# Transposes of sums moved from TensorE to VectorE, a separate list for block loads, and the split maxima turned later in the step

## The reference

```python
x = x + _L0_xattn_ref(_layernorm(x), ctx, ctx)       # gelu(x ctx^T) ctx, 1601 rows of ctx per batch
x = x + _L0_ffn_ref(_layernorm(x), Wg, W1, W2)       # 8 experts of 512, each token to one of them
x = x + _L1_xattn_ref(ctx, _layernorm(x), mask, Wq, Wk, Wv, Wo, rel_bias)
x = x + _L1_ffn_ref(_layernorm(x), Wp1, ..., Wo, bo) # one expert per batch, chosen from its last row
```

```python
q = (dst @ Wq.T).reshape(B, T_q, H, D_K)             # H = 16 heads of D_K = 16
scores = einsum('bqhd,bkhd->bhqk', q, k) + bias
scores = where(mask, scores, -1e9)
out = einsum('bhqk,bkhd->bqhd', softmax(scores), v).reshape(B, T_q, H * D_K)
return out @ Wo.T
```

## Time and profile before

| | |
|---|---|
| median of 3 runs | 728.78 us (727.0 to 732.06) |
| the profiled execution | 730.0 us |
| its span | 728.1 us |
| TensorE busy | 652.9 us (90%) |
| VectorE busy | 336.9 us (46%) |
| ScalarE busy | 272.0 us (37%) |
| mean clock of TensorE | 0.966 of full |

### The profile page before, as it was taken

The page is one execution under the profiler, slowest core; times in us unless marked ns, Lnnn a source line. Parts: engine busy times, 40 slices in busy tenths (PEclk is TensorE's granted clock), DMA queues, the critical chain, the costliest instruction groups (busy, mean ns, idle before and its releaser), DMA issues.

```text
span 728.1 us, 9151 instructions
## 1 busy us (share of the span) xinstructions
PE 652.9 (90%) x3116; PEld 392.0 (54%) x3117; DVE 336.9 (46%) x1093; ACT 272.0 (37%) x375; POOL 97.1 (13%) x101
## 2 busy tenths in 40 slices
PE   3999999999997767999976899999999989899996
PEld 2666666666664446999864333334334334344644
DVE  4324423003026872232236776777777767323302
ACT  1111111111121330434305576675775766752220
POOL 0000000000020002445520613000102300303000
PEclk9999999999998996999989899999999989999999
DMA  9992205203001135122254760560462000402031
GB/s 310 361 361 99 95 1 169 77 0 120 0 1 63 35 106 152 50 65 66 78 149 56 104 88 2 80 99 27 79 93 62 3 2 2 117 1 59 5 110 59
DMA packets 48100, 61.98 MB, mean 85 GB/s; under 512 B 7927, under 2 KB 41240, under 8 KB 47656
## 3 DMA queue, kind: packets, MB, share of 16 engines
q1 hardware_dynamic: 45944, 55.66, 29.3%
q0 software_dynamic: 2112, 5.77, 2.8%
HBM read 43.89 MB, written 10.93 MB: 75 GB/s over the span
## 4 chain that ended last, share of the span: by engine, by line
PE 71%; DVE 14%; issue 5%; DMA 5%; ACT 3%; POOL 1%; POOLq 0%; DVEq 0%; ACTq 0%; SPq 0%
PE ps L860 13%; PE ps L871 12%; PE ps L1430 7%; PE ps L1412 5%; PE ps L1300 5%; PE ps L1132 4%; PE ps L1123 3%; DVE arena L2122 3%; PE ps L1028 3%; DVE arena L1830 2%; PE ps L944 2%; PE ps L1142 2%; PE ps L1020 2%; PE ps L1097 2%; PE ps L1333 2%
## 5 line engine op out<-in xcount | busy, mean ns | idle before, releaser
L2122 DVE TENSOR_REDUCE arena<-ps 128x1 f32<-128x400 f32 x256 | 130.9, 566 | 49.7 <-PE ps L1300 49.0
L1652 ACT ACTIVATE arena<-ps 100x1024 f32<-100x1024 f32 x128 | 124.3, 1022 | 57.4 <-PE ps L1412 57.2
L860 PE MATMUL ps<-xnT,arena 128*128 128x512 f32 x208 | 102.0, 616 | 0.9 <-DVE xnT L1715 0.9
L871 PE MATMUL ps<-arena 128*128 128x256 f32 x416 | 98.5, 381 | 0.0
L871 PEld LDWEIGHTS ps<-arena 128*128 128x128 f32 x416 | 79.6, 191 | 32.8 <-issue 24.5
L1475 ACT ACTIVATE arena<-ps 128x512 f32<-128x512 f32 x52 | 31.0, 597 | 174.9 <-PE ps L860 174.9
L1300 PE MATMUL ps<-arena 97*128 97x400 bf16 x256 | 76.4, 342 | 6.3 <-ACT xnT L1613 2.0
L1412 PE MATMUL ps<-arena 100*100 100x512 bf16 x256 | 77.7, 388 | 1.1 <-DMA arena<-arena 0.6
L1430 PE MATMUL ps<-arena 100*32 100x512 f32 x512 | 70.6, 615 | 0.2 <-ACT arena L1652 0.2
L1300 PEld LDWEIGHTS ps<-arena 97*128 97x128 bf16 x256 | 20.4, 97 | 78.7 <-DVE arena L2122 38.9
L1715 DVE COPY xnT<-ps 128x512 f32<-128x512 f32 x16 | 10.4, 686 | 100.9 <-PE ps L833 100.9
(11 more groups left out here) (228 smaller groups left out, 717.4 us busy)
## 6 DMA issues: line engine op xcount, KB each, us to landing
arena<-in_W SPq DMA_DIRECT2D x16, 512.0 KB, 9.1
arena<-in_ctxT SPq DMA_DIRECT2D x4, 1664.0 KB, 7.9
arena<-in_ctxN SPq DMA_DIRECT2D x4, 1664.0 KB, 12.9
arena<-arena SPq DMA_DIRECT2D x48, 128.0 KB
arena<-in_pW SPq DMA_DIRECT2D x8, 512.0 KB, 4.4
last_k_parts<-arena SPq DMA_DIRECT2D x24, 100.0 KB, 1.8
arena<-last_k_parts SPq DMA_DIRECT2D x8, 300.0 KB
x_tok<-in_x SPq DMA_DIRECT2D x4, 512.0 KB, 9.3
```

Of the source, the lines that this page charges most:

```text
L860: ins = pe.matmul(ps[:, 4 + k % 2, :], ctxT_s[:, b % 2, c, f * P:f * P + P], xnT[:, c, S * b:S * b + S], start=(c == 0), stop=(c == KC - 1))
L871: ins = pe.matmul(ps[:, b % 2 * 2 + t // 2, t % 2 * D:t % 2 * D + D], hid[:, (k - 2) % 4, t * P:t * P + P], ctxN_s[:, b % 2, f, :], start= ...
L1652: act.activation(pexp2[0:KT, c % 4, :, :], ps[0:KT, 2 + 2 * (c % 2):4 + 2 * (c % 2), :], ACT.Exp).then_inc(f_pe, 1)
L2122: dve.tensor_reduce(nm2[:, h, j:j + 1], ps[:, FAST.bank(x), 0:KF], AX.X, ALU.max, negate=True).then_inc(s_by["dve"], 1)
```

## The change

1. **Sums.** In `fast_way` VectorE now transposes the sums itself, in squares of 32 x 32 elements, straight from bank 6 into `vt2`, in the first step of the next unit. One square is a head's 32 rows by 32 queries, so the sum of exponentials of a query ends up beside its values. In the second step it divides into `vn2`, and in the third step of every second unit it transposes 128 x 512 of them back into `xnT`. The copies by ScalarE, the transposes on TensorE and the turning of the finished batch ("turn", "last turn") go; `WoT` is laid out for the new order of columns on the host. The batch is projected at steps 3 and 4, its roots begin at step 4, and "turn4" stands at 10 and 12.
2. **Maxima.** The split maxima are transposed at the end of the second step, behind its sum product and its last two maxima products, instead of ahead of the sum product. ScalarE takes them last in the step.
3. **Experts.** The list of tokens to load is made by itself after the block transposes (`s_idxl`); GpSimd issues each load as soon as that block is turned, then the stores. `s_ysd` goes; the engines wait for the stores themselves. A row of zeros is stored once ahead of the loop. SyncE loads the first keys only after the first four gathers (`s_xsb` 64).
4. **Threshold.** One of the key products stands behind the transpose of the threshold.
5. **End of attention.** The last batch's projection stands ahead of the first answers of the fourth block, on TensorE and on VectorE.

The general way (`near > 0`), which these inputs don't take, is adapted to the new order of columns.

```diff
-CHAIN = {3: ("turn", 0), 4: ("turn", 1), 7: ("project", 0), 8: ("project", 1), 12: ("turn4", 0), 15: ("turn4", 1)}
+CHAIN = {3: ("project", 0), 4: ("project", 1), 10: ("turn4", 0), 12: ("turn4", 1)}
+ROOTS_AT = 4
...
-    if t == 1 and u + 1 < UNITS:
-        found.append(("max rows", u + 1))
-    if t == 2 and u >= 1:
-        found.append(("values", u - 1))
...
+def rows_of_step(st):
+
+    u, t = divmod(st, CT)
+    return u + 1 if t == 1 and u + 1 < UNITS else None
...
             sp.wait_ge(s_ekst[0], 48 * KC * B // 2)
+            sp.wait_ge(s_xsb, 64)
             for half in range(2):
                 keys(0, half)
...
-                last_keys(3 + r)
+                if r + 1 < ROUNDS:
+                    last_keys(3 + r)
             pe.wait_ge(s_soft, 3)
             pe.transpose(ps[:, 0, 0:P], kept[:, CAND:CAND + 1].broadcast_to([P, P]), eye).then_inc(s_prT, 1)
+            last_keys(2 + ROUNDS)
...
                         max_products(maxima_of_step(st, 2, HG))
+                        if rows_of_step(st) is not None:
+                            turn_maxima(rows_of_step(st))
...
-                part4_hidden(0, 0, 2)
-                turn_values(UNITS - 1)
-                part4_hidden(0, 2, FC)
+                part4_hidden(0, 0, FC)
+                pe.wait_ge(f_oc, UNITS)
                 route_logits(FAST, 1)
                 pe.wait_ge(s_acc_f, B)
-                pe.wait_ge(f_oc, UNITS)
-                for k in range(KC):
-                    turn_piece(FAST, ("last turn", B - 1, k))
                 pe.wait_ge(f_pe, 2 * STEPS)
+                project(B - 1, 4)
                 reasoned(0, 0)
-                for k in range(KC):
-                    taken(FAST, ("last turn", B - 1, k))
-                project(B - 1, 4)
                 reasoned(0, 1)
...
-                    act.wait_ge(s_ysd, i + 1)
+                    act.wait_ge(s_ys, i * 32 + 16)
...
-                    if st % CT == 0 and st > 0:
-                        take_values(st // CT - 1)
...
+                dve.wait_ge(s_xsTr, i * 2 + 3)
+                dve.tensor_scalar(idx_x[:, :], idx[:, bass.ds(i * 2 + 4, 2)], 0.0, None, ALU.add).then_inc(s_idxl, 1)
                 for j in range(2):
                     dve.wait_ge(s_xsTr, i * 2 + j + 3)
                     dve.tensor_copy(xsT[:, j, :, :].rearrange("p k n -> p (k n)"), ps[:, 6 + j, 0:KC * P]).then_inc(s_xsT, 1)
-                dve.tensor_scalar(idx_x[:, :], idx[:, bass.ds(i * 2 + 4, 2)], 0.0, None, ALU.add)
-                dve.wait_ge(s_ysd, i + 1)
+                dve.wait_ge(s_ys, i * 32 + 16)
                 dve.tensor_scalar(idx_y[:, :], idx[:, bass.ds(i * 2, 2)], 0.0, None, ALU.add).then_inc(s_idx, 1)
...
+                def turn_values(i):
+
+                    dve.wait_ge(f_pv, CT * (i + 1))
+                    dve.transpose(vt2[:, i % 2, :, :].rearrange("p a v -> p (a v)"), ps[:, 6, :]).then_inc(f_oc, 1)
+
                 def normalise(i):
 
-                    b, g = divmod(i, NG)
-                    x = ("values", i)
-                    dve.wait_ge(s_made, FAST.made(x))
-                    v = ps[:, FAST.bank(x), :].rearrange("p (j h v) -> p j h v", j=TB, h=HG)
-                    cf.step(dve, dve.reciprocal(rl2[:, :, :, :], v[:, :, :, DK:DK + 1]))
-                    dve.tensor_tensor(xn[:, TB * b:TB * b + TB, g * HG * DK:(g + 1) * HG * DK].rearrange("p t (h d) -> p t h d", d=DK),
-                                      v[:, :, :, 0:DK], rl2.broadcast_to([P, TB, HG, DK]), ALU.mult).then_inc(s_by["dve"], 1)
...
+                    lo = i % 2 * DK
+                    dve.wait_ge(f_oc, i + 1)
+                    cf.step(dve, dve.reciprocal(rl2[:, :, :], vt2[:, i % 2, :, DK:DK + 1]))
+                    cf.step(dve, dve.tensor_tensor(vn2[:, i // 2 % 2, :, lo:lo + DK], vt2[:, i % 2, :, 0:DK],
+                                                   rl2.broadcast_to([P, S // VW, DK]), ALU.mult))
+
+                def turn_back(i):
+
+                    b, k = divmod(i // 2, KC)
+                    ins = dve.transpose(xnT[:, k, S * b:S * b + S], vn2[:, k, :, :].rearrange("p a v -> p (a v)"))
...
+                    if t == 0 and u >= 1:
+                        turn_values(u - 1)
+                    if t == 1 and u >= 1:
+                        normalise(u - 1)
+                    if t == 2 and u >= 1 and u % 2 == 0:
+                        turn_back(u - 1)
...
-                        n = st - (b + 1) * NG * CT - 7
+                        n = st - (b + 1) * NG * CT - ROOTS_AT
...
             with pool.Fori(0, pairs) as i:
+                pool.wait_ge(s_idxl, i + 1)
+                pool.sem_inc(s_turn, 1)
+                for j in range(2):
+                    pool.wait_ge(s_xsTr, i * 2 + j + 3)
+                    pool.sem_inc(s_turn, 1)
+                    load_tokens(j, idx_x[:, j:j + 1])
                 pool.wait_ge(s_idx, i + 1)
                 pool.sem_inc(s_turn, 1)
-                for j in range(2):
-                    load_tokens(j, idx_x[:, j:j + 1])
...
-                pool.wait_ge(s_ys, i * 32 + 32)
-                pool.sem_inc(s_ysd, 1)
```

More of the change, by code:

```diff
@@ L183, in maxima_of_step @@
     return range(min(first + lo, UNITS * MU), min(first + hi, UNITS * MU))
-TAKER = {"max": "dve", "max rows": "act", "values": "dve", "queries": "act", "products": "act", "turn": "act", "project": "dve",
-         "turn4": "act", "route": "act", "logits": "dve", "last turn": "dve", "last turn4": "dve"}
+TAKER = {"max": "dve", "max rows": "act", "queries": "act", "products": "act", "project": "dve",
+         "turn4": "act", "route": "act", "logits": "dve", "last turn4": "dve"}
 LAST_TURNS = [(("last turn4", B - 1, 0), 6), (("last turn4", B - 1, 1), 7), (("route", 2), 6), (("logits", 2), 4)]
@@ L214, in fast_pieces @@
             yield ("max", m), next(turns), TAKER["max"]
-    for name, bank in [(("route", 1), 7), (("values", UNITS - 1), 7), (("logits", 1), 6), (("last turn", B - 1, 0), 6),
-                       (("last turn", B - 1, 1), 7)] + LAST_TURNS:
+        if rows_of_step(st) is not None:
+            yield ("max rows", rows_of_step(st)), next(turns), TAKER["max rows"]
+    for name, bank in [(("route", 1), 7), (("logits", 1), 6)] + LAST_TURNS:
         yield name, bank, TAKER[name[0]]
@@ L555, in _ @@
         def _(sp):
-            for s_free in (s_ysd, s_kst, s_mr):
+            for s_free in (s_kst, s_mr):
                 sp.sem_inc(s_free, 1)
@@ L2204, in fast_way @@
                         split_maxima(u + 1)
+                turn_values(UNITS - 1)
                 normalise(UNITS - 1)
+                turn_back(UNITS - 1)
                 route_shift(FAST, 1)
-                for k in range(KC):
-                    take_turned(FAST, ("last turn", B - 1, k))
-                answers(0, 0)
                 choose(1)
                 project(B - 1, 4, 1)
+                answers(0, 0)
                 answers(0, 1)
```

62 lines of the change are left out of this document (25 added, 37 removed).

## The result

The changed kernel takes 747.26 us, the median of four runs (745.93 to 748.77), against 728.5 for the kernel before on the same chip: the ratio is 1.025 (95% interval 1.0209 to 1.0291). It is slower, by far more than the 1% that a measurement can tell, and outside the range of 710 to 728. The profiled execution has a span of 745.8 us, 17.7 more than the one before.

What follows compares the result with a forecast made beforehand. TensorE was taken to set the attention loop's pace, VectorE not far behind; the expert head waits for a gather. Terms -6.3 - 2.9 + 1.3 - 1.8 = -9.7 gave 719 us for the median, range 710 to 728.

Steps and rivals of the forecast that it cites:

- (a): Head of expert stage: gather freed from key loads, start 3.7 us earlier, first hidden products 2.6 us shorter; -6.3 us.
- (b): Expert loop: fetch list made and loads issued earlier, so nine passes take 67.5 us instead of 70.4; -2.9 us.
- (c): Threshold turned before a key product: the product delays the prefix sums by what the threshold gained; 0.
- (e): End of attention: the last sums' turning and last rows' transposes with their wait leave TensorE; -1.8 us.
- (d): Attention loop: turning moved from TensorE to VectorE; +2.1 us at full clock, -0.8 for the clock, +1.3 us in all.
- The walk: Step-by-step queue timing of attention: clean unit 12.2 us against 11.97, batch 56.9 against 55.0; sum +2.8, less 0.7.
- the crowd: Unit with the second projection: first step 5.1 us on VectorE against TensorE's 4.4; TensorE stands still 1.9 us.
- the clock: Rival: three long TensorE waits each bring several us at 1.2 GHz, more near the router; attention +9, whole 727; chance 0.10.

Runs made afterwards that it cites:

- e1: Kernel before with only parts 3 and 4 of the change (experts, threshold), attention loop untouched: ratio 0.993 to the kernel before.
- e2: Changed kernel with the second projection, statistics, roots and turned rows of a batch spread over more steps: ratio 0.9949 to the kernel before.
- e9: As e5, with GpSimd's additions to the first batch's rows moved behind those of the second: ratio 0.9745 to the kernel before.
- e10: As e9, with SyncE loading the first keys only after eight gathers instead of four: ratio 0.9762 to the kernel before.
- e3: Changed kernel with filler products on TensorE at its waits in the unit of the second projection: ratio 1.0156 to the kernel before.
- e4: Changed kernel with GpSimd's two additions per batch cut to one column of 256 (result not the reference's): ratio 1.0073 to the kernel before.
- e5: As e2, with late queries one step and their products two steps earlier, and a GpSimd wait ahead of its additions: ratio 0.9812 to the kernel before.
- e6: Kernel before (TensorE turns sums) with the change's expert stage and threshold, maxima's transposes behind the sum product, late products earlier: ratio 0.9891 to the kernel before.
- e8: The changed kernel run again, code identical: ratio 1.023 to the kernel before.
- e11: Changed kernel with projections, roots and turned rows at their old steps: ratio 1.0136 to the kernel before.
- e7: Kernel before with only the maxima's transposes moved behind the sum product: ratio 0.9959 to the kernel before.

## Why the prediction was wrong

- **(a) Head, -6.3.** Half right. The start moved by 4.4 us (3.7 forecast). The first hidden products took 5.44 us, not 3.7, at a clock of 0.69: the fall came with the shorter wait too in this execution, as in e1, e2, e9 and e10, and not in e3, e4, e5, e6, e8 and e11 (3.81 there). I had read the fall of the kernel before as one that came while TensorE waited; it came right behind: the clock was 1.00 from 281 to 285 us and 0.64 in the two us after. And "I take nothing" for the key loads meeting the first pass's gathers was wrong: 1.43 us here, up to 3.5 in others. By the third pass 3.7 us were left (301.04 against 304.74).
- **(b) Passes, -2.9.** Right in this execution: from the third pass to the end of the last answers 60.4 us against 62.8, -2.4. It did not come again: the same code took 64.7 us in e8, and e7, with the old expert stage on the same chip, 65.4. In e8 and every other run with this expert stage some passes took 8.3 or 8.4 us with an idle time of 0.5 at their start that the profile puts down to no wait; why, is open.
- **(c)** nothing seen, as said. **(e) -1.8:** right, -1.6.
- **(d) Attention, at full clock.** The walk was good: clean unit 12.08 for 12.2, transposes 0.717 for 0.69 to 0.71, the crowd where it was put. The second batch of e8, which has no fall, took 56.0 us, where the walk had 56.9 and the kernel before takes 54.9; its longest wait of TensorE was 1.39 us, not 1.9. e7 came out to 0.1 us, with a stretch of 3.4 us at 1.2 GHz gone besides, and e9's loop 3 us under the walk's 208 for its table of steps. Over the whole loop the 2.1 us that it forecast as lost at full clock are not to be seen in the balance below.
- **(d) Attention, the clock.** The step that failed is "I count two clock falls of 1.2 us: +2.4 - 3.2 = -0.8". Against what the same steps take in e4, e5 and e8 the changed kernel loses 6.1 us at steps 8 to 10, 4.5 at 20 to 22, 3.4 and 7.8 in the third batch (the second of these is GpSimd's), 4.5 at 52 to 54 and 3.0 at the end, 29.3 in all; less the 3.2 us that the kernel before itself lost that makes 26.1 of the 25.6 measured, so the queues at full clock cost about nothing in sum. About 6 of the 29.3 are the three waits for GpSimd themselves (1.47, 2.78 and 1.74 us), an estimate, and the other 23 the clock. Both factors were wrong. The **price** of a fall is 4.5 us, not 1.2: no row gives 1.2, and the kernel before lost 3.2 at two short stretches of 6.8 and 3.4 us, 1.6 each, while in five of the six places here the clock stayed low for 10 to 14 us. And the **number** was six, not two: the crowd that I foresaw gave three, and three more came because the waits at them had a cause that I didn't have, VectorE's small operations held until GpSimd's instruction ended.
- The prediction has no term for GpSimd at all: what its instructions do to VectorE's stood at nothing without a reason. The rival named "the clock" had the mechanism, with "several us" for each long wait, and the size of +9 for it was a third of what came. Its price of 727 was 20 us too low. The sign of GpSimd's part was in the trace of before: in the unit at 452 us the casts of the split took 0.59 and 1.01 us beside GpSimd's, for a TensorE wait of 1.20.

## What to carry to other kernels

Where TensorE is busy nine tenths of the time, a wait of 1.4 us, or two of 0.54 and 0.74 close together (at 625 us), can cost 4.5 us of clock, and need not (e3, e8); so ask of a change that moves work to another engine which are the longest waits that it makes in one place, not what it adds to the sum. List the small operations of VectorE whose duration varies, and lay GpSimd's instructions over them in the timeline: an engine for which nobody waits can still hold the chain. Filler products in a suspected wait are a cheap test of whether the clock or the queue is what costs.

## What was not expected of the hardware

- Of the 31 stretches at 1.2 GHz in the table, 18 went on for 10.2 to 23.9 us with TensorE busy nearly throughout (8.00 of 8.00 us in two windows of e5), behind single idle times of 1.1 to 2.9 us or two of 0.5 and 0.7 close together. The Trainium skill, "TensorE: Matmul & The Clock Gate", section "Part 1: The HAM clock gate (the "warmup" mystery)", lets it return to full clock much sooner under sustained work; the traces here don't agree.
- The same order of the same instructions fell at different places in two executions (e8), with the total within 0.2% as a ratio.
- VectorE's product of 128x4 elements took 0.16 us alone and up to 2.04 beside GpSimd's addition in the changed kernel; the transpose of 128x512 out of PSUM (0.72) and the maxima were not held.
